# Gathering one chunk of every eleventh group with SyncE in two softmax passes of a graph network

## The chip, the cores and the metric

The kernel runs on one core of a Trainium2 chip as a single launch. The metric is the device time of one execution in microseconds, the median of several. PE is TensorE (PEld its weight loads), DVE VectorE, ACT ScalarE, POOL GpSimd and SP SyncE.

## The reference, cut to what matters

Four graph layers run over 6250 nodes with 128 features and 100,000 edges, each followed by a residual sum and a layer norm. The change touches layers 1 and 2. Both fetch one row per edge from a table that is indexed by the edge's source, take a softmax over the edges of each destination, and sum the weighted rows per destination:

```python
# layer 1 (eight heads; keys kt and values vt by edge type)
kt = jnp.einsum('nhi,thij->tnhj', k, relation_att)[edge_type, src]
e = (q[dst] * kt).sum(-1) * relation_pri[edge_type] * scale
m = jax.ops.segment_max(e, dst, num_segments=n)
ex = jnp.exp(e - m[dst])
a = ex / jax.ops.segment_sum(ex, dst, num_segments=n)[dst]
vt = jnp.einsum('nhi,thij->tnhj', v, relation_msg)[edge_type, src]
agg = jax.ops.segment_sum(a[..., None] * vt, dst, num_segments=n)
# layer 2 (four heads; one table x_l)
e = jax.nn.leaky_relu(x_l[src] + x_r[dst], NEG_SLOPE)
logits = jnp.einsum('ehc,hc->eh', e, att)
...
out = jax.ops.segment_sum(alpha[:, :, None] * x_l[src], dst, num_segments=n)
```

## The kernel before

The kernel sorts the edges by destination and pads them to 832 chunks (`CH`) of 128 edges. Four chunks (`G`) make a group, so a pass has 208 groups (`GROUPS`). `read_order` reads the sorted list back and makes, for each chunk, a column of row numbers: `by_dst.typed` (edge type times 6400 plus source, for layer 1) and `by_dst.other` (the source, for layer 2).

`softmax_pass` is one block of straight code per engine, unrolled over the groups. In layer 1 a fetched row has 256 floats (keys and values, from the table `related`), in layer 2 it has 132 (from `left_table`). The queues divide the work in this way:

- POOL issues one indirect DMA per chunk (L1505), four per group, into `rows`, a ring of 11 groups in layer 1 and 15 in layer 2. Before group n it waits until DVE has weighed group n - ring, which DVE does at the end of its step n - 1.
- DVE runs one step per group: it makes the one-hot matrix of group n (L140), multiplies group n - 2 with its spread queries (L1788 in layer 1, L1791 in layer 2), reduces to scores (L1814), weighs an older group (L1877) and adds older sums to `total` (L1694). Every `wg` groups (4 in layer 1, 8 in layer 2) a window's running maximum is formed by scans on DVE and small transposes on PE, and this work is spread over the steps of the following window.
- PE transposes the one-hots, spreads the queries (L1582; in layer 2 it also adds the fetched rows, L1585, and so waits for the gather itself) and sums the weighted rows (L1610). ACT casts between them.
- SP loads the break table in 32 DMAs (64 in layer 2) at the pass's start (L1479), and then, in layer 1, waits for the last score and reloads `k.x` (L1492). Nothing else stands on its queue.

A group's four gathers count on one semaphore, `got[slot]`, which the readers await at a fixed multiple. Each DMA adds 16 to its semaphore. All numbers of a wait are fixed when the program is built.

Of the kernel before, what the change touches and what calls it, by code (L numbers as in the profile page):

```python
# [5 lines left out]
ALU = mybir.AluOpType  # L6
# [4 lines left out]
I32 = mybir.dt.int32  # L11

P = 128
# [8 lines left out]
G = 4  # L22
# [14 lines left out]
GROUPS = CH // G  # L37
# [9 lines left out]
SPAN = TU + NBLK  # L47
assert PAD_STEP * (CH - 1) + PAD_SKIP * (P - 1) < N
AFTER = NSLOT - E
assert TU * QU == CU and RING * G == 64 and NBLK < (RING - 2) * G  # L50

NBD = NBLK + NBLK % 2
NPD = NBD * P
# [75 lines left out]
def load_blocks(nc, engine, chunk, count, most=NBLK - 1):  # L129

    _, regs = nc.values_load_multi_w_load_instructions(
        chunk, engines=[engine], min_val=0, max_val=most,
        skip_runtime_bounds_check_because="the table is clamped to the last block")
    return regs
# [596 lines left out]
                pool.wait_ge(sent[s], 64 * (groups // SLOTS))  # L731


def read_order(nc, k, table, o, breaks, fields, name, stack=None, shared=None):


    with ExitStack() as own:
# [5 lines left out]
        starts = sb("starts", [TQ, QT, P])  # L743
        breaks_sb = sb("breaks_sb", [TQ, QT, P], BF16)
        end = sb("end", [1, P], BF16)
        outs = [out for _, out in fields] + [o.begins]
        turned = ps("turned", [P, 4, 512])
        loaded = [sem(f"loaded{h}") for h in range(2)]
# [12 lines left out]
        @block.sync  # L761
        def _(sp):
            for h in range(2):
                here = slice(h * half, (h + 1) * half)
                sp.dma_start(lst[:, here, :], rows[:, here, :]).then_inc(loaded[h], 16)
            sp.dma_start(before[:], rows_before).then_inc(led, 16)
            sp.wait_ge(ended, 1)
            sp.dma_start(breaks[NSLOT:NSLOT + P].rearrange("(a b) -> a b", a=1), end[:]).then_inc(stored, 16)
            sp.wait_ge(flagged, 2)
            sp.dma_start(breaks[0:NSLOT].rearrange("(q p e) -> p q e", q=QT, e=P), breaks_sb[:]).then_inc(stored, 16)  # L770
            sp.wait_ge(stored, 32)

        @block.tensor
        def _(pe):
# [584 lines left out]


def softmax_pass(nc, k, o, index, table, row, head, values_at, spread, att, peaks, total, reload, loops, wg, name, beside=(),
                 ringed=False):

# [18 lines left out]
    with ExitStack() as ctx:  # L1384
# [71 lines left out]
        rescaled = sem("rescaled")  # L1456
        reloaded = sem("reloaded")
        kept = sem("kept")
        block = ctx.enter_context(nc.Block())
        slots = GROUPS + lag + 2  # L1460
        last_own = GROUPS + 1 - lag
# [12 lines left out]
        @block.sync  # L1474
        def _(sp):
            for n, here in enumerate((slice(0, batch), slice(batch, windows))):
                count = here.stop - here.start
                for s in range(strips):
                    sp.dma_start(brk[s * heads:(s + 1) * heads, here, :],  # L1479
                                 brk_h[s * length:s * length + NSLOT].rearrange("(a w l) -> a w l", a=1, l=wch * P)  # L1480
                                 [:, here, 0:length + 1].to_broadcast([heads, count, length + 1])).then_inc(loaded[n], 16)
            for tile, home, inward in beside:
                sp.dma_start(*((tile, home) if inward else (home, tile))).then_inc(kept, 16)
            for n in range(GU if ringed else 0):
                sp.wait_ge(got[n % RING], (n // RING + 1) * 16 * G)
                sp.sem_inc(landed, 1)
            if beside:
                sp.wait_ge(kept, 16 * len(beside))
            if reload is not None:
                tile, home = reload  # L1490
                sp.wait_ge(scored, GROUPS)
                sp.dma_start(tile, home).then_inc(reloaded, 16)  # L1492
                sp.wait_ge(reloaded, 16)

        @block.gpsimd
        def _(pool):
            for n in range(GU if ringed else GROUPS):
                s = n % ring
                if n >= ring:

                    pool.wait_ge(weighed if at else scored, n - ring + 1 + (NBLK // G if ringed else 0))
                    pool.sem_inc(running, 1)
                for g in range(G):
                    c = n * G + g
                    nc.gpsimd.indirect_dma_start(rows[:, s, g, :], None, table,  # L1505
                                                 bass.IndirectOffsetOnAxis(ap=index[:, c:c + 1], axis=0),
                                                 ).then_inc(got[s], 16)
# [48 lines left out]
        def _(pe):  # L1556
# [4 lines left out]
            for n in range(slots):  # L1561
# [10 lines left out]
                if 0 <= t < GROUPS:  # L1572
                    b = t % 2
                    blocks = load_blocks(nc, pe.engine, o.block[:, t * G:(t + 1) * G], G)

                    pe.wait_ge(copied, t + 1)
                    if t >= 2:
                        pe.wait_ge(paired, t - 1)
                    if att is not None:
                        pe.wait_ge(got[t % ring], (t // ring + 1) * 16 * G)  # L1580
                    for g in range(G):
                        last = nc.tensor.matmul(own[:, b, g, :], onehot_t[:, b, g, :], spread[:, bass.ds(blocks[g], 1), :],  # L1582
                                                start=True, stop=(att is None))
                        if att is not None:
                            last = nc.tensor.matmul(own[:, b, g, :], k.ident[:], rows[:, t % ring, g, 0:D],  # L1585
                                                    start=False, stop=True)
                    last.then_inc(spread_ok, 1)
# [74 lines left out]
        def _(dve):  # L1662
# [33 lines left out]
            for n in range(slots + 1):  # L1696
# [2 lines left out]
                m = n - lag  # L1699
                if n >= GROUPS + 2:  # L1700
                    add_sums(n - lag - 2)
                if n < GROUPS:
                    if n >= hots:

                        dve.wait_ge(widened, n - hots + 1)
                    mark(nc, onehot[:, n % hots, :, :], numbers, o.place[:, n * G:(n + 1) * G]).then_inc(hot, 1)
# [61 lines left out]
                if 0 <= t < GROUPS:  # L1768
                    b = t % 2

                    if ringed:
                        slots_of = load_blocks(nc, dve.engine, o.slot[:, t * G:(t + 1) * G], G, RING * G - 1)
                        need = dve.value_load(o.need[:, t:t + 1], min_val=1, max_val=GU)
                        dve.wait_ge(landed, need)
                    else:
                        dve.wait_ge(got[t % ring], (t // ring + 1) * 16 * G)
                    dve.wait_ge(spread_ok, t + 1)
                    if t >= 2:
                        dve.wait_ge(scored, t - 1)
# [1353 lines left out]
def graph_network(nc, a, out):  # L3133
    k = Shared()
    k.semaphores = []
    with ExitStack() as ctx:
        def sb(name, shape, dt=F32):
            return ctx.enter_context(nc.sbuf_tensor(f"k_{name}", shape, dt))
# [23 lines left out]
        by_src.gather = sb("src_gather", [P, CU], I32)  # L3162
        by_src.slot, by_src.need = sb("src_slot", [1, CH], I32), sb("src_need", [1, GROUPS], I32)
        by_src.free = sb("src_free", [1, 2 * P], I32)
        by_dst.typed = sb("dst_typed", [P, CH + SPARE], I32)
        by_dst.other = sb("dst_other", [P, CH + SPARE], I32)
        relational = ctx.enter_context(ExitStack())
# [9 lines left out]
        with ExitStack() as sort:  # L3177
# [51 lines left out]
            with unblocked as dense:  # L3229
                def tmp(name, shape, dt=F32):  # L3230
# [28 lines left out]
                swap_in(nc, k, queries, x_home, shared, "l1_swap")  # L3259
                read_breaks(nc, k, by_src.sorted, by_src, by_src.breaks, "src_breaks", dense, shared)  # L3260
            read_order(nc, k, by_dst.sorted, by_dst, by_dst.breaks,
                       [(1, by_dst.other), (2, by_dst.typed), (0, by_dst.place)], "dst_read")
            free_semaphores(nc, k)
        with ExitStack() as layer:
            total = layer.enter_context(nc.sbuf_tensor("l1_total", [P, NBLK - 1 + G, D + HEADS1], F32))
            softmax_pass(nc, k, by_dst, by_dst.typed, related.rearrange("t n f -> (t n) f"), 2 * D, D // HEADS1, D,
                         k.x, None, False, total, (k.x[:], x_home), None, 4, "l1_pass")
            relation_output(nc, k, total, a["L1_gnn_w_basis_a"], a["L1_gnn_loop_weight"], a["L1_gnn_bias"], mix,
                            "l1_out")
        relational.close()  # L3270
# [3 lines left out]
        with ExitStack() as layer:  # L3274
            def tmp(name, shape, dt=F32):
                return layer.enter_context(nc.sbuf_tensor(f"l2_{name}", shape, dt))

            right = tmp("right", [P, NBD, D])
            total = tmp("total", [P, NBLK - 1 + G, D + 2 * HEADS2])
            left = total[:, 0:NBD, 0:D + HEADS2]  # L3280
            loop_scores = tmp("loop_scores", [P, NBD, HEADS2])
            norm_project(nc, k, w2[:], None, [(0, D + HEADS2, left, 1.0), (D + HEADS2, 2 * D + HEADS2, right, 1.0)], [(left, left_table)], "l2_project")
            softmax_pass(nc, k, by_dst, by_dst.other, left_table, D + HEADS2, D // HEADS2, 0, right, att_row[:], True, total,
                         None, (left, loop_scores, k.x[:], bias2[:]), 8, "l2_pass")
            attention_output(nc, k, total, loop_scores, left_table, "l2_out")

        free_semaphores(nc, k)
# [44 lines left out]
```

## Time and profile before

| | |
|---|---|
| median of 3 runs | 9749.5 us (9728.2 to 9752.75) |
| profiled execution | 9737.26 us, span of its trace 9735.5 us |
| POOL busy | 6993.0 us (72%) |
| DVE busy | 6539.5 us (67%) |
| PE busy | 6374.2 us (65%) |
| ACT busy | 2118.1 us (22%) |

The span is cut into stretches by lines of the program: layer 1's pass runs from about 5188 to 6275 us and layer 2's from about 6429 to 7500 us. A line of a group gives the engine, the operation and its count, the duration of one in ns (least, median, most) and when the first and the last started. Lines indented under it say what ended the engine's idle time before it, or who waited for it, with the sum in us and the number of times. A name that ends in q (SPq, PEldq) is that engine's instruction queue: DMA issues and register instructions stand there and are not counted as busy.

### The profile page before, as it was taken

The numbers are of one execution on the slowest core, as the hardware profiler recorded it, in microseconds if no ns is written. First come the engines' busy times: TensorE is split into PE (matmuls) and PEld (weight loads), VectorE is DVE, ScalarE is ACT, GpSimd is POOL, SyncE is SP. The second block draws the span as 40 slices with busy tenths as digits, with TensorE's granted clock in tenths as the row PEclk, the third lists the DMA queues.
The fourth block names the chain that finished last, engine by engine and source line by source line (L and its number), as shares of the span: only waits on it lengthen the run. The fifth ranks groups of instructions, "written<-read, shape, count | busy, mean of one in ns | idle before, by whom it ended". The sixth has DMA issues, their size and how long they took to land. (4 is left out here: it accounts for less than half of the span.)

```text
span 9735.5 us, 171552 instructions
## 1 busy us (share of the span) xinstructions
PE 6374.2 (65%) x37681; PEld 5551.4 (57%) x37682; DVE 6539.5 (67%) x22695; ACT 2118.1 (22%) x6216; POOL 6993.0 (72%) x7418
## 2 busy tenths in 40 slices
PE   6777655547666577639404666767776688876666
PEld 5666544436655566634204666556675578766665
DVE  7555566668777777736305888877777666667777
ACT  5222100001111111112101222232222222223333
POOL 7777777767777777777776777547775577767775
PEclk7555555556666655569756888889999665667777
DMA  0000012122212212234303333222222322223333
GB/s 25 2 2 2 18 53 52 53 61 53 53 53 55 57 53 53 53 77 146 100 2 86 104 104 104 87 47 55 55 55 55 100 54 54 54 72 108 108 108 97
DMA packets 436037, 614.74 MB, mean 63 GB/s; under 512 B 176561, under 2 KB 312069, under 8 KB 435109
## 3 DMA queue, kind: packets, MB, share of 16 engines
q0 software_dynamic: 257024, 486.93, 19.6%
q1 hardware_dynamic: 178305, 119.49, 4.3%
q8 instruction: 183, 3.00, 0.1%
q10 hardware_dynamic: 292, 3.41, 0.1%
q14 instruction: 233, 1.91, 0.1%
HBM read 520.17 MB, written 89.19 MB: 63 GB/s over the span
## 5 line engine op out<-in xcount | busy, mean ns | idle before, releaser
L1179 PE MATMUL hop_sums<-hop_rows,hop_weighted 128*128 x4992 | 1152.1, 403 | 1053.2 <-SPq L1315 674.4
L1128 POOL DMA_INDIRECT hop_rows<-hops,k_src_gather x1568 | 1483.3, 946 | 486.8 <-issue 477.6
L1179 PEld LDWEIGHTS hop_sums<-hop_rows,hop_weighted 128*128 128x128 f32 x4992 | 989.6, 295 | 1158.8 <-issue 1158.7
L1505 POOL DMA_INDIRECT l_pass_rows<-left_table,k_dst_other x832 | 796.2, 957 | 433.2 <-issue 244.6
L1505 POOL DMA_INDIRECT l_pass_rows<-related,k_dst_typed x832 | 788.6, 948 | 308.6 <-issue 238.7
L1505 POOL DMA_INDIRECT l_pass_rows<-key_table,k_src_gather x784 | 744.3, 949 | 365.9 <-issue 234.8
L2000 POOL DMA_INDIRECT l_weigh_rows<-row_table,l_weigh_ring x832 | 790.0, 949 | 297.9 <-issue 213.1
L728 POOL DMA_INDIRECT src_sorted<-src_scatter_records,src_scatter_places x784 | 753.1, 961 | 260.4 <-issue 188.2
L1355 POOL DMA_INDIRECT dst_sorted<-rec,dst_places x768 | 752.8, 980 | 237.2 <-issue 237.2
L1128 POOL DMA_INDIRECT hop_rows<-in_x,k_src_gather x784 | 742.4, 947 | 249.0 <-issue 238.7
L1213 DVE TENSOR_SCALAR hop_weighted<-k_numbers,k_src_place,src_weight 128x128 f32<-128x128 f32 x2496 | 850.1, 403 | 15.7 <-issue 8.7
L1521 ACT CAST l_pass_onehot_t<-l_pass_turned 128x512 f32<-128x512 bf16 x624 | 365.7, 586 | 2158.6 <-PE l_pass_turned L1569 2110.8
L1600 PE MATMUL l_pass_sums<-l_pass_zero 128*128 128x272 bf16 (+1 forms) x1210 | 235.7, 279 | 465.2 <-DVE l_total L1694 322.0
L1582 PE MATMUL l_pass_own<-l_right,l_pass_onehot_t 128*128 x1664 | 359.0, 299 | 257.7 <-DMA l_pass_rows<-left_table,k_dst_other 243.8
L1610 PE MATMUL l_pass_sums<-l_pass_terms,l_pass_onehot_f 128*128 128x136 f32 x3232 | 513.1, 308 | 1.1 <-DVE l_pass_terms L1877 1.1
L664 PE MATMUL src_scatter_nexts<-src_scatter_next_sb,src_scatter_oh_lo_t 128*128 128x50 f32 x1568 | 494.2, 425 | 0.0
L1106 ACT COPY hop_next_sb<-hop_next_ps 128x50 f32<-128x50 f32 x784 | 158.1, 202 | 1522.6 <-PE hop_next_ps L1151 1516.5
L1610 PEld LDWEIGHTS l_pass_sums<-l_pass_terms,l_pass_onehot_f 128*128 128x128 f32 x3232 | 472.1, 217 | 26.3 <-issue 3.2
L2018 PE MATMUL l_weigh_own<-l_keys,l_weigh_onehot_t 128*128 x1672 | 321.5, 352 | 229.9 <-ACT l_weigh_onehot_t L1970 229.9
L1814 DVE TENSOR_REDUCE l_pass_scores<-l_pass_pair 128x32 f32<-128x512 f32 (+1 forms) x624 | 426.2, 683 | 14.5
L1582 PEld LDWEIGHTS l_pass_own<-l_right,l_pass_onehot_t 128*128 128x128 f32 x1664 | 267.1, 202 | 289.7 <-issue 289.7
L2018 PEld LDWEIGHTS l_weigh_own<-l_keys,l_weigh_onehot_t 128*128 128x128 f32 x1672 | 272.4, 247 | 274.6 <-issue 274.6
(477 smaller groups left out, 17048.9 us busy)
## 6 DMA issues: line engine op xcount, KB each, us to landing
related<-l_tables_rows SPq DMA_DIRECT2D x50, 1024.0 KB, 4.5
hop_rows<-hops,k_src_gather POOLq DMA_INDIRECT x1568
l_pass_rows<-related,k_dst_typed POOLq DMA_INDIRECT x832
l_pass_rows<-left_table,k_dst_other POOLq DMA_INDIRECT x832
l_weigh_rows<-row_table,l_weigh_ring POOLq DMA_INDIRECT x832
src_sorted<-src_scatter_records,src_scatter_places POOLq DMA_INDIRECT x784, 2.1
hop_rows<-in_x,k_src_gather POOLq DMA_INDIRECT x784, 2.5
dst_sorted<-rec,dst_places POOLq DMA_INDIRECT x784
```

The lines of the kernel that those rows point to most:

```text
L664: nc.tensor.matmul(nexts[:, b, g, 0:HIS], oh_lo_t[:, b, g, :], next_sb[:, g % 2, :], start=True, stop=True).then_inc(looked, 1)
L728: nc.gpsimd.indirect_dma_start(table, bass.IndirectOffsetOnAxis(ap=places[:, s, g:g + 1], axis=0), records[:, s, g, :], None).then_inc(sen ...
L1128: nc.gpsimd.indirect_dma_start(rows[:, s * G + g, :], None, table_in, bass.IndirectOffsetOnAxis(ap=o.gather[:, c:c + 1], axis=0),).then_in ...
L1179: last = nc.tensor.matmul(sums[:, b, g, :], weighted[:, s % SLOTS, g, :], rows[:, bass.ds(slots[g], 1), :], start=True, stop=True)
L1213: last = nc.vector.tensor_scalar(weighted[:, s, g, :], k.numbers, o.place[:, c], o.weight[:, c], ALU.is_equal, ALU.mult)
L1355: nc.gpsimd.indirect_dma_start(table, bass.IndirectOffsetOnAxis(ap=places[:, c:c + 1], axis=0), rec[:, c, :], None).then_inc(sent[c % SLOT ...
L1505: nc.gpsimd.indirect_dma_start(rows[:, s, g, :], None, table, bass.IndirectOffsetOnAxis(ap=index[:, c:c + 1], axis=0),).then_inc(got[s], 16)
L1582: last = nc.tensor.matmul(own[:, b, g, :], onehot_t[:, b, g, :], spread[:, bass.ds(blocks[g], 1), :], start=True, stop=(att is None))
L1610: last = nc.tensor.matmul(into[:, bass.ds(within[g], 1), 0:width], onehot_f[:, m % 2, g, :], term, start=False, stop=False, skip_group_che ...
L1814: nc.vector.tensor_reduce(mine, pair[:, b, :, :, :].rearrange("p (s t) h f -> p s t h f", t=per), AX.X, ALU.add).then_inc(scored, 1)
L2000: nc.gpsimd.indirect_dma_start(rows[:, s, g, :], None, table, bass.IndirectOffsetOnAxis(ap=ring[:, s, g:g + 1], axis=0),).then_inc(got[s], 16)
L2018: last = nc.tensor.matmul(own[:, b, g, :], onehot_t[:, b, g, :], spread[:, bass.ds(blocks[g], 1), :], start=True, stop=True)
```

## The change

Groups 16, 27, ... 203 of each pass (18 of 208) are side groups. POOL issues three gathers for them instead of four, 814 per pass in all. Their last chunk is fetched by SP: it loads the chunk's 128 row numbers from DRAM into `side_list`, takes eight at a time into registers, and issues 128 DMAs of one row each into `side`, a tile with two buffers. At step n of a side group DVE waits for the 128 rows and copies them to their place in `rows`; PE and DVE wait for this copy (`side_in`) before they use the group. SP may refill a buffer when DVE has copied the one before it. The row numbers by chunk come from `read_order`, where POOL computes them from the list and SP stores them in two DRAM tables.

```diff
+FIRST_SIDE, SIDE_STEP = 16, 11
+AT_ONCE = 8
...
# read_order, SP (after the breaks are stored) and POOL
-            sp.wait_ge(stored, 32)
+            sp.wait_ge(homed, 4)
+            for tile, home in ((other_i, other_home), (typed_i, typed_home)):
+                sp.dma_start(home.rearrange("(q p) e -> p q e", q=QT), tile[:]).then_inc(stored, 16)
+            sp.wait_ge(stored, 64)
+        @block.gpsimd
+        def _(pool):
+            for h in range(2):
+                pool.wait_ge(loaded[h], 16)
+                nc.gpsimd.tensor_copy(other_i[:, here, :], by_edge[:, here, :, 1]).then_inc(homed, 1)
+                nc.gpsimd.tensor_scalar(first_row[:, here, :], by_edge[:, here, :, 2], float(NPD), None, ALU.mult).then_inc(first_ok, 1)
...
+                nc.gpsimd.tensor_copy(typed_i[:, here, :], first_row[:, here, :]).then_inc(homed, 1)
# softmax_pass, SP
+            def list_side(j):
+                c = side_groups[j] * G + G - 1
+                sp.dma_start(side_list[:, j % 2, :], row_home[c:c + 1, :]).then_inc(side_listed[j % 2], 16)
+            for j in range(2 if side_groups else 0):
+                list_side(j)
+            for j, n in enumerate(side_groups):
+                b = j % 2
+                sp.wait_ge(side_listed[b], 16 * (j // 2 + 1))
+                if j >= 2:
+                    sp.wait_ge(side_in, j - 1)
+                for first in range(0, P, AT_ONCE):
+                    nodes = load_blocks(nc, sp.engine, side_list[:, b, first:first + AT_ONCE], AT_ONCE, table.shape[0] - 1)
+                    for e, node in enumerate(nodes):
+                        sp.dma_start(side[first + e:first + e + 1, b, :], table[bass.ds(node, 1), :]).then_inc(side_got[b], 16)
+                if j + 2 < len(side_groups):
+                    list_side(j + 2)
# softmax_pass, POOL
-                for g in range(G):
+                for g in range(G - 1 if n in side_groups else G):
# softmax_pass, PE before L1582 and DVE before L1788 and L1791
-                        pe.wait_ge(got[t % ring], (t // ring + 1) * 16 * G)
+                        pe.wait_ge(got[t % ring], gathered(t))
+                        if t in side_groups:
+                            pe.wait_ge(side_in, side_groups.index(t) + 1)
# softmax_pass, DVE at the start of step n
+                if n in side_groups:
+                    j = side_groups.index(n)
+                    dve.wait_ge(side_got[j % 2], (j // 2 + 1) * 16 * P)
+                    if n >= ring:
+                        dve.wait_ge(weighed, n - ring + 1)
+                    nc.vector.tensor_copy(rows[:, n % ring, G - 1, :], side[:, j % 2, :]).then_inc(side_in, 1)
```

On SP, from the end of `read_order` into layer 1's pass, these instructions stood in a row before (`x16` is a run of 16 alike; `dst_read_breaks_sb` are the breaks of the sorted list, `l_pass_brk` the pass's table of them):

```order
L770 DMA dst_breaks<-dst_read_breaks_sb 104x8x128
L737 UNCONDITIONAL_BRANCH
L1474 UNCONDITIONAL_BRANCH
L1479 DMA l_pass_brk<-dst_breaks 8x4x129 x16
L1479 DMA l_pass_brk<-dst_breaks 8x48x129 x16
L1492 DMA k_x<-x_home 128x6400
L1384 UNCONDITIONAL_BRANCH
```

Now the stores of the two tables and the row fetches stand between them; `ISA` is a register instruction that turns a row number into an address:

```order
L778 DMA dst_breaks<-dst_read_breaks_sb 104x8x128
L781 DMA dst_other_home<-dst_read_other_i 104x8x128
L781 DMA dst_typed_home<-dst_read_typed_i 104x8x128
L739 UNCONDITIONAL_BRANCH
L1510 UNCONDITIONAL_BRANCH
L1515 DMA l_pass_brk<-dst_breaks 8x4x129 x16
L1515 DMA l_pass_brk<-dst_breaks 8x48x129 x16
L1528 DMA l_pass_side_list<-dst_typed_home 1x128 x2
L133 TENSOR_LOAD l_pass_side_list
L1541 ISA
L1541 DMA l_pass_side<-related 1x256
L1541 ISA
```

The last two rows come 128 times per side group, with one load of eight numbers ahead of every eight, and 18 such blocks stand ahead of the reload of `k_x`.

On DVE, step 16 of layer 1's pass began in this way before:

```order
L1694 TENSOR_TENSOR l_total<-l_total,l_pass_sums 128x544
L131 TENSOR_LOAD k_dst_by_chunk
L1914 ISA
L1914 SCALAR_TENSOR_TENSOR l_total<-l_pass_small,l_total 128x128
L1917 ISA
L1917 SCALAR_TENSOR_TENSOR l_total<-l_pass_small,l_total 128x8
L140 TENSOR_TENSOR l_pass_onehot<-l_pass_numbers,k_dst_place 128x512
```

Now the copy out of the side tile stands ahead of the one-hot:

```order
L1751 TENSOR_TENSOR l_total<-l_total,l_pass_sums 128x544
L133 TENSOR_LOAD k_dst_by_chunk
L1980 ISA
L1980 SCALAR_TENSOR_TENSOR l_total<-l_pass_small,l_total 128x128
L1983 ISA
L1983 SCALAR_TENSOR_TENSOR l_total<-l_pass_small,l_total 128x8
L1765 COPY l_pass_rows<-l_pass_side 128x256
L142 TENSOR_TENSOR l_pass_onehot<-l_pass_numbers,k_dst_place 128x512
```

The one-hot, and all that DVE has queued behind it, moved behind the wait of this copy.

## Rows read from the trace of the kernel before

**Rows 1.** POOL's gathers, line L1505, in layer 1's pass, then layer 2's:

```profile
L1505 POOL DMA_INDIRECT l_pass_rows<-related,k_dst_typed x832: 941/949/985, 5188.4 to 6251.5; - x167
  issue: 238.7, 756
  DVE l_pass_terms L1877: 36.7, 75
...
  DVE l_pass_pair L1788: 20.2, 8
...
L1505 POOL DMA_INDIRECT l_pass_rows<-left_table,k_dst_other x832: 941/947/6695, 6429.9 to 7481.0; - x167
  DVE l_pass_terms L1877: 11.2, 31
...
  PE l_pass_own L1582: 243.8, 165
```

**Rows 2.** DVE's one-hots, line L140, steps 16 to 203, layer 1, layer 2:

```profile
L140 DVE TENSOR_TENSOR l_pass_onehot<-l_pass_numbers,k_dst_place x188: 672/680/684, 5268.9 to 6226.3; 128x512 bf16<-128x512 f32 x188
L140 DVE TENSOR_TENSOR l_pass_onehot<-l_pass_numbers,k_dst_place x188: 671/681/685, 6516.4 to 7455.1; 128x512 bf16<-128x512 f32 x188
```

**Rows 3.** Windows: busy us of PE, PEld, DVE, ACT, POOL; PEclk, DMA share, GB/s:

```profile
5269.00:6226.00 957.00, 668.91 (x4672) 601.55 (x4670) 773.31 (x1919) 247.71 (x655) 709.20 (x749) 0.84 0.36 104
6517.00:7455.00 938.00, 701.42 (x5886) 645.69 (x5886) 697.00 (x1493) 276.58 (x794) 707.87 (x749) 0.98 0.25 55
```

**Rows 4.** SP's waits: us in total, times, longest:

```profile
SPq L1492 <- DVE l_pass_scores L1814: 1019.8, 1, 1019.8
```

**Rows 5.** Lines of SP's, PE's and ACT's queues: DMA issues and register instructions:

```profile
L1479 SPq DMA_DIRECT2D l_pass_brk<-dst_breaks x32: 268/298/308, 6429.2 to 6439.8; - x32
L1479 SPq DMA_DIRECT2D l_pass_brk<-dst_breaks x16: 264/301/363, 5187.7 to 5193.0; - x16
L2436 SPq FUSED_REGOPS  x50: 46/46/51, 4422.6 to 4732.1; - x50
L2436 SPq DMA_DIRECT2D related<-l_tables_rows x50: 372/372/409, 4422.7 to 4732.3; - x50
L1318 SPq TENSOR_LOAD <-k_src_free x540: 262/267/465, 1217.1 to 4126.8; - x180
L131 PEldq TENSOR_LOAD <-k_dst_by_chunk x1041: 326/331/345, 5198.0 to 9680.2; - x174
L1173 PEldq TENSOR_LOAD <-k_src_need x624: 305/310/322, 1198.8 to 4163.2; - x156
L295 ACTq DMA_DIRECT2D dst_sorted<-dst_load_pad x1: 305/305/305, 138.4 to 138.4; - x1
```

**Rows 6.** DMA queues (packets, MB, share), 5248:5249, 5249:5260, 6461:6462, 6462:6475, 6428:6441:

```profile
q1 hardware_dynamic: 20, 0.00, 2.2%
...
q0 software_dynamic: 424, 1.15, 35.8%
...
q1 hardware_dynamic: 10, 0.00, 1.1%
...
q0 software_dynamic: 307, 0.63, 22.0%
...
q1 hardware_dynamic: 375, 0.07, 2.6%
```

**Rows 7.** DMA issues: KB each, median us from issue to landing:

```profile
weights_att_column<-in_L_gnn_att SPq DMA_DIRECT2D x1, 0.5 KB, 2.2
```

**Rows 8.** DVE's groups by form: busy us, mean ns of one, idle:

```profile
L2727 DVE COPY l_right<-l_project_product 128x256 f32<-128x256 f32 x25 | 10.4, 414 | 0.0
```

**Rows 9.** POOL's own arithmetic, two lines, and SP's store of the breaks:

```profile
L347 POOL TENSOR_SCALAR src_count_oh_lo<-k_count,src_keys x196: 597/612/694, 15.4 to 131.0; 128x128 bf16<-128x128 f32 x196
L220 POOL IOTA src_load_slot_no<- 128x832 int32 x1 | 0.8, 827 | 0.7 <-POOLq L156 0.7
...
5183.68 0.30 SPq L770 DMA_DIRECT2D dst_breaks<-dst_read_breaks_sb  x1
5187.74 51.95 SPq L1479 DMA_DIRECT2D l_pass_brk<-dst_breaks  x32
```

More of the change, by code:

```diff
@@ L731, in _, with read_order @@
                 pool.wait_ge(sent[s], 64 * (groups // SLOTS))
-def read_order(nc, k, table, o, breaks, fields, name, stack=None, shared=None):
+def read_order(nc, k, table, o, breaks, fields, other_home, typed_home, name, stack=None, shared=None):
     with ExitStack() as own:
@@ L745, in read_order @@
         end = sb("end", [1, P], BF16)
+        other_i = sb("other_i", [TQ, QT, P], I32)
+        typed_i = sb("typed_i", [TQ, QT, P], I32)
+        first_row = sb("first_row", [TQ, QT, P])
+        homed = sem("homed")
+        first_ok = sem("first_ok")
+        row_ok = sem("row_ok")
         outs = [out for _, out in fields] + [o.begins]
@@ L770, in _ @@
             sp.dma_start(breaks[0:NSLOT].rearrange("(q p e) -> p q e", q=QT, e=P), breaks_sb[:]).then_inc(stored, 16)
-            sp.wait_ge(stored, 32)
+            sp.wait_ge(homed, 4)
[5 more added lines that the diff above has]
+            for h in range(2):
+                here = slice(h * half, (h + 1) * half)
+                pool.wait_ge(loaded[h], 16)
+                nc.gpsimd.tensor_copy(other_i[:, here, :], by_edge[:, here, :, 1]).then_inc(homed, 1)
+                nc.gpsimd.tensor_scalar(first_row[:, here, :], by_edge[:, here, :, 2], float(NPD), None, ALU.mult).then_inc(first_ok, 1)
+                pool.wait_ge(first_ok, h + 1)
+                nc.gpsimd.tensor_tensor(first_row[:, here, :], first_row[:, here, :], by_edge[:, here, :, 1],
+                                        ALU.add).then_inc(row_ok, 1)
+                pool.wait_ge(row_ok, h + 1)
+                nc.gpsimd.tensor_copy(typed_i[:, here, :], first_row[:, here, :]).then_inc(homed, 1)
         @block.tensor
@@ L1361, in softmax_pass @@
 def softmax_pass(nc, k, o, index, table, row, head, values_at, spread, att, peaks, total, reload, loops, wg, name, beside=(),
-                 ringed=False):
+                 ringed=False, row_home=None):
     heads = D // head
@@ L1458, in softmax_pass, with gathered @@
         kept = sem("kept")
+        side_groups = range(FIRST_SIDE, GROUPS, SIDE_STEP) if row_home is not None else ()
+        if row_home is not None:
+            side = sb("side", [P, 2, row])
+            side_list = sb("side_list", [1, 2, P], I32)
+            side_listed = [sem(f"side_listed{b}") for b in range(2)]
+            side_got = [sem(f"side_got{b}") for b in range(2)]
+            side_in = sem("side_in")
+        def gathered(n):
+            return sum(16 * (G - 1 if before in side_groups else G) for before in range(n % ring, n + 1, ring))
         block = ctx.enter_context(nc.Block())
@@ L1775, in _ @@
                     else:
-                        dve.wait_ge(got[t % ring], (t // ring + 1) * 16 * G)
+                        dve.wait_ge(got[t % ring], gathered(t))
+                        if t in side_groups:
+                            dve.wait_ge(side_in, side_groups.index(t) + 1)
                     dve.wait_ge(spread_ok, t + 1)
@@ L3164, in graph_network @@
         by_src.free = sb("src_free", [1, 2 * P], I32)
+        by_dst.other_home, by_dst.typed_home = dram("dst_other_home", [CH, P], I32), dram("dst_typed_home", [CH, P], I32)
         by_dst.typed = sb("dst_typed", [P, CH + SPARE], I32)
@@ L3261, in graph_network @@
             read_order(nc, k, by_dst.sorted, by_dst, by_dst.breaks,
-                       [(1, by_dst.other), (2, by_dst.typed), (0, by_dst.place)], "dst_read")
+                       [(1, by_dst.other), (2, by_dst.typed), (0, by_dst.place)], by_dst.other_home, by_dst.typed_home, "dst_read")
             free_semaphores(nc, k)
@@ L3266, in graph_network @@
             softmax_pass(nc, k, by_dst, by_dst.typed, related.rearrange("t n f -> (t n) f"), 2 * D, D // HEADS1, D,
-                         k.x, None, False, total, (k.x[:], x_home), None, 4, "l1_pass")
+                         k.x, None, False, total, (k.x[:], x_home), None, 4, "l1_pass", row_home=by_dst.typed_home)
             relation_output(nc, k, total, a["L1_gnn_w_basis_a"], a["L1_gnn_loop_weight"], a["L1_gnn_bias"], mix,
@@ L3283, in graph_network @@
             softmax_pass(nc, k, by_dst, by_dst.other, left_table, D + HEADS2, D // HEADS2, 0, right, att_row[:], True, total,
-                         None, (left, loop_scores, k.x[:], bias2[:]), 8, "l2_pass")
+                         None, (left, loop_scores, k.x[:], bias2[:]), 8, "l2_pass", row_home=by_dst.other_home)
             attention_output(nc, k, total, loop_scores, left_table, "l2_out")
```

## The prediction

> **What bounds the kernel now.** I read the line of the gathers on POOL in each pass first, because that is the work the change takes away, and its waits before its busy time. In both passes POOL issues 832 gathers of about 0.948 us with some 0.306 us of issue between two (244.6 us over 800, or 238.7 over 756), 1.25 us apiece and 5.0 us a group [rows 1]. The reader is to see who ends whose wait. In layer 2 PE waits 243.8 us, 165 times, for a gather to land, while POOL waits for DVE only 11.2 us. POOL's issue sets that pass. In layer 1 it is the other way round: POOL waits 75 times for DVE's weighing, 36.7 us in all, while DVE waits for gathers 8 times, 20.2 us [rows 1]. There DVE's chain of steps sets the pace.
>
> The steps of DVE say the same. From step 16 to step 203, the first and last side group, layer 1 takes (6226.3 - 5268.9)/187 = 5.12 us a step, more than POOL's 5.0; layer 2 takes (7455.1 - 6516.4)/187 = 5.02, POOL's pace [rows 2]. DVE is busy 773 of 957 us in the one and 697 of 938 in the other [rows 3]; layer 2 has room on DVE, layer 1 little. SP is free: in layer 1's pass it stands in one wait of 1019.8 us [rows 4].
>
> **What POOL gives back.** 18 x 1.25 = 22.5 us per pass is the most. In layer 2 it is all worth having if nothing else becomes late; in layer 1 it is worth nothing, since POOL already waits for DVE there.
>
> **What a side chunk costs SP.** This is the term that decides. Per row SP runs one register instruction and one DMA issue. The register instruction with multiplications takes 46 ns at L2436 [rows 5]. A DMA issue that need not wait for its predecessor took 264 and 268 ns, the least of the two runs of small issues; in the run of 32 most took 298 at a pitch of (6439.8 - 6429.2)/31 = 342 ns, so 44 ns lie between two instructions [rows 5]. With a register instruction between, each issue starts some 400 ns after the last, later than that pitch, so I take 270 ns and not 298. A row is 270 + 44 + 46 + 44 = 404 ns, and 128 rows are 51.7 us. The load of one number takes SP 267 ns; on PE four numbers take 331 where one takes 310, so eight cost about 49 more than one, 267 + 49 + 44 = 360 ns, 16 times 5.8 us. The issue of the next list is 0.3. A chunk costs SP C = 57.8 us.
>
> DVE's own pace for 11 steps is 11 x 5.12 = 56.3 us in layer 1 and 11 x 5.02 = 55.2 in layer 2. SP is the slower of the two by a little, and then DVE waits for SP at every side group, and everything behind DVE's copy in its queue (one-hot, products, weighing) waits, so PE, ACT and POOL too.
>
> Bounds for C, from the rows on both sides: if the register instruction hides behind the pitch, a row is 342 ns and C = 49.9; if every issue takes the 301 of the run of 16 (nearly the 305 of the one-partition store on ACT), a row is 435 and C = 61.8. A 128-partition issue took 372, another kind of transfer; it would make C = 70.9 and is the far end.
>
> A page would make it dearer. The Trainium skill, DMA: Bandwidth & Descriptors, section Latency and other measured facts, puts a register load at 600 ns at least; that would add 16 x 0.33 = 5.3 us to C and 36 x 5.3 = 191 us to the time. Here 540 loads on SP took 262 ns and up [rows 5], so the trace disagrees and I leave it out.
>
> **When SP can begin.** The row lists stand behind the break table in SP's DMA queue. In layer 1 the last packets of that queue move in 5248 to 5249 and none after 5249; in layer 2 the last move in 6461 to 6462 [rows 6]; q1 is SP's queue and has no row in the later windows. I begin the rows at 5249.5 and 6462.5, and add 2.2 us for the last row to land, as for a load of 0.5 KB [rows 7].
>
> **The sum.** If SP sets the pace, the copy of the last side group can start at begin + 18 C + 2.2.
> - Layer 1: 5249.5 + 1040.4 + 2.2 = 6292.1, against step 203 at 6226.3: 65.8 us later. DVE's own pace would be less: first rows at 5309.5 (a stall of 40.6 at step 16), then 17 x 56.7 us, to 6273.4. So SP decides, and +66.
> - Layer 2: 6462.5 + 1040.4 + 2.2 = 7505.1 against 7455.1: +50. POOL's 22.5 us are lost in this wait.
> - The copies: 128x256 took DVE 0.41 us out of another memory [rows 8]; 36 of at most that are 15 us, but all but one per pass lie inside the waits for SP. +0.5 us.
> - `read_order`: POOL runs eight passes over 512 numbers. The near rows are 827 ns for 832 numbers and 612 for 128 [rows 9], so 0.5 to 2.4 us each, 4 to 20 in all, in the shadow of DVE's work up to the store at 5183.68 or past it. Then two stores of 425 KB follow the store of the breaks, half that size, for which the block had 4.06 us up to the pass's first issue at 5187.74 [rows 9]. +1 to +10; I take +4, near the first row, which is a plain stream.
> - PE's and DVE's new waits on `side_in` stand two steps behind the copy and cost nothing. DVE's wait on `weighed` is for its own last step. The bytes fetched stay the same.
>
> Together 66 + 50 + 0.5 + 4 = +120 us. On the profiled execution's 9737.3 us (9735.5 of span and 1.8 around it) that is 9857; it ran 12 us under the median of 9749.5, so I predict 9870.
>
> **Rivals.**
>
> (a) SP keeps up. At C = 49.9 the first rows land at 5301.6 in layer 1, and DVE then goes at its own 56.7: 5301.6 + 963.9 = 6265.5, +39. In layer 2 they land at 6514.6, ahead of step 16 at 6516.4; POOL sets the pace and the whole 22.5 us are gained. With `read_order` +39 + 1 - 22.5 + 4 = +21, that is 9770, not slower than a measurement can tell. If POOL's relief counted in layer 1 as well, it would be -1, 9748. The point from which this case decides is C = 54 or less, 373 ns a row; for it speaks that a single issue can be as cheap as 264, against it that something has to stand between two. C = 54.4 gives +43 - 11 + 4 = +36.
>
> (b) One DMA ring is the limit, not SP's issue. Each row is one descriptor with its own completion. If these finish one behind the other in more than 404 ns, C is 128 times that. At 800 ns a row C = 102.4, and both passes end 18 x 44.6 us later still: 9870 + 1606 = 11,476. Against it: of the 32 small transfers with 384 packets (eight pieces and four counts each) 375 moved, with other ones', in the 13 us around their issue [rows 6], so transfers at 342 ns do not pile up there. But they may lie on several rings, and the rows show no transfer of one descriptor in a row of many. [...]
>
> (c) The side path is ready early and both passes are freed: -22.5 in each and +4, 9708. It needs the stall at step 16 of layer 1 gone, that is the first 128 rows in 19 us, 150 ns a row, under every row seen, and POOL's relief to count in layer 1, where POOL waits. I give it almost nothing.
>
> **How the numbers follow.** A measurement of this kernel can tell 0.3%, 29 us, from no change. SP as the bound with C from 54.4 to 62 (9785 to 10,020): 0.66. Still dearer issue, up to the far end, by hiccups or by 372 ns an issue: C = 66 gives 18 x 8.2 x 2 = 295 us more than the forecast, 10,165: 0.10. Rival (b): 0.08. Rival (a): 0.13. Rival (c): 0.03. Each us on C moves the time 36 us, and this makes the range: from 9770 (rival a) to 10,060 (C = 63), leaving the upper cases out. Slower by over 0.3%: 0.66 + 0.10 + 0.08 = 0.84; within: 0.13; faster: 0.03.
>
> **What would show it.** In the profile after, a row fetch on SP at a pitch of 400 ns and 18 blocks of some 58 us back to back; DVE's copy waiting for SP's DMA about 40 us at step 16 of layer 1 and about 5 in layer 2, then 1 to 3 us at each side group; POOL's waits for DVE grown in both passes; steps 16 to 203 about 983 us long in layer 1. The forecast is wrong if SP stands in its wait for `side_in` (it keeps up), if SP's blocks are short but the rows land late (ring), or if TensorE's granted clock, 0.98 of full speed in layer 2 [rows 3], falls towards its lower level of 1.2 GHz when PE idles more, which I have not priced.

## The result, and the profile after

The changed kernel takes 10,197.0 us, the median of 5 runs (10,192.6 to 10,198.8). The kernel before took 9744.2 us beside it (5 runs, 9728.2 to 9752.75). The ratio is 1.0464, 95% interval 1.0452 to 1.0476: 453 us slower. The forecast of 9870 us had the sign and the mechanism, and fell short of the size by almost three quarters of the loss. The profiled execution of the changed kernel took 10,198.8 us (its trace spans 10,197.1), 2 above the median; that of the kernel before, 9737.3 (9735.5), lies 7 below its own.

The steps of DVE come first, as in [rows 2]: its one-hots, steps 16 to 203, layer 1 and layer 2 (count, least/median/most ns of one, first and last start in us).

```profile
L142 DVE TENSOR_TENSOR l_pass_onehot<-l_pass_numbers,k_dst_place x188: 672/680/685, 5319.9 to 6462.1; 128x512 bf16<-128x512 f32 x188
L142 DVE TENSOR_TENSOR l_pass_onehot<-l_pass_numbers,k_dst_place x188: 671/681/692, 6763.7 to 7905.7; 128x512 bf16<-128x512 f32 x188
```

One of them takes what it took, 0.68 us, but the 187 steps last 1142.2 and 1142.0 us, where they lasted 957.4 and 938.7. The two layers had a pace of their own before; now both have the same one, 6.11 us a step or 67.2 us for eleven. Something that does not know the layer sets it. What DVE waits for stands under the copy of the side rows, with the idle time ahead of it and its number of waits:

```profile
L1765 DVE COPY l_pass_rows<-l_pass_side x36: 229/262/294, 5319.7 to 7905.5; 128x256 f32<-128x256 f32 x18, 128x132 f32<-128x132 f32 x18
...
  DMA l_pass_side<-left_table: 264.3, 18
  DMA l_pass_side<-related: 236.7, 18
```

DVE waits for SP's rows at every one of the 36 side groups, 501.0 us in all. The longest wait is at step 16 of layer 1; the waits of DVE in that stretch give it (total, times, longest), and below it the one of layer 2:

```profile
DVE l_pass_rows L1765 <- DMA l_pass_side<-related: 59.1, 2, 46.8
...
DVE l_pass_rows L1765 <- DMA l_pass_side<-left_table: 13.4, 1, 13.4
```

Then SP itself, in one block of 128 rows of layer 1, 5319 to 5387 us: the load of eight row numbers (L133) and what it runs for each row (L1541).

```profile
L133 SPq TENSOR_LOAD <-l_pass_side_list x17: 715/780/926, 5319.0 to 5386.3; - x17
...
L1541 SPq FUSED_REGOPS  x128: 37/37/37, 5319.8 to 5385.5; - x128
L1541 SPq MOVE l_pass_side<-related x128: 29/29/29, 5319.9 to 5385.6; - x128
L1541 SPq DMA_DIRECT2D l_pass_side<-related x128: 224/225/260, 5319.9 to 5385.6; - x128
```

The 128 rows go out in 65.7 us, and the 17th load is already the next block's: the blocks stand back to back, 67.2 us apart. A row starts 0.408 us after the last (median; 0.42 in the mean, with a gap of some 0.3 us more here and there). A load of eight takes 780 ns, and the two rows around it start 1.21 us apart, so it adds 0.80 us to the row's 0.408. POOL, relieved of 18 gathers a pass, stands and waits (line as in [rows 1], with the idle time ahead of it):

```profile
L1560 POOL DMA_INDIRECT l_pass_rows<-related,k_dst_typed x814: 942/949/1048, 5192.3 to 6486.7; - x163
...
  DVE l_pass_terms L1943: 279.6, 84
...
L1560 POOL DMA_INDIRECT l_pass_rows<-left_table,k_dst_other x814: 939/947/6763, 6664.0 to 7930.9; - x163
...
  DVE l_pass_terms L1943: 240.2, 55
```

Its waits for DVE grew from 36.7 to 279.6 us and from 11.2 to 240.2. The stretches of steps 16 to 203 in both layers (busy us of PE, PEld, DVE, ACT and POOL, then PEclk, DMA share and GB/s, as in [rows 3]):

```profile
5320.00:6462.00 1142.00, 707.26 (x4674) 632.37 (x4674) 776.85 (x1935) 247.72 (x655) 692.95 (x731) 0.76 0.31 87
6764.00:7906.00 1142.00, 733.54 (x5891) 674.05 (x5891) 699.63 (x1511) 276.58 (x794) 691.39 (x731) 0.88 0.20 46
```

Beside SP, no engine has much more to do than before. DVE, which now makes the copies, is busy 3.5 and 2.6 us longer. PE does the same matmuls in 38 and 32 us more, at a lower granted clock (0.84 to 0.76, 0.98 to 0.88 of full speed).

The loss adds up. From the start of a pass to its last score, layer 1 went from 1071.8 to 1303.9 us (+232.1) and layer 2 from 1057.4 to 1273.3 (+215.9); from `read_order`'s first load to layer 1's first issue it went from 21.96 to 28.98 (+7.0). That is 455 of the 461.6 us between the two traces; the medians are 453 apart. The other 6.6 lie in stretches that the change does not touch: what follows layer 2's last score took 2248.9 us before and 2260.5 after, and between 2251.6 and 2270.7 in five kernels of the experiments.

### The profile page after: what moved, and what is told of

The parts are those of the page before. It is cut to its first block and busy times, and to the rows that moved or that the text cites. A ratio compares the mean times of both kernels' runs of the same rounds, so it can differ in the third digit from the quotient of the medians.

```text
span 10197.1 us, 186120 instructions
## 1 busy us (share of the span) xinstructions
PE 6487.5 (64%) x37681; PEld 5652.8 (55%) x37682; DVE 6548.0 (64%) x22731; ACT 2118.3 (21%) x6216; POOL 6973.3 (68%) x7390
## 5 line engine op out<-in xcount | busy, mean ns | idle before, releaser
L1560 POOL DMA_INDIRECT l_pass_rows<-related,k_dst_typed x814 | 771.7, 948 | 534.2 <-DVE l_pass_terms L1943 279.6
L1624 PE MATMUL l_pass_turned<-k_identb,l_pass_onehot 128*128 128x128 bf16 x2496 | 302.7, 258 | 512.5 <-DVE l_pass_onehot L142 511.6
L1624 PEld LDWEIGHTS l_pass_turned<-k_identb,l_pass_onehot 128*128 128x128 bf16 x2496 | 210.2, 118 | 538.5 <-DVE l_pass_onehot L142 524.0
L1177 PE MATMUL hop_nexts<-hop_next_sb,hop_oh_lo_t 128*128 128x50 f32 x1568 | 439.0, 379 | 0.0
```

What stands on the lines that cost most here:

```text
L1177: nc.tensor.matmul(nexts[:, b, g, 0:HIS], oh_lo_t[:, b, g, :], next_sb[:, g % 2, :], start=True, stop=True).then_inc(looked, 1)
L1624: last = nc.tensor.transpose(turned[:, g, :], onehot[:, n % hots, g, :], k.identb[:])
```

## The experiments

The question was why a block costs SP 67.2 us and not 57.8, whether it is SP alone that holds the passes up, and what is left of the gain when SP does not. The kernel before took 9745.6 us (median) beside the first four and 9749.1 beside the last three.

**`mixed`: what a load costs by its size.** The side chunks load 1, 2, 4, 8 and 16 numbers at a time, in turn.

```diff
-AT_ONCE = 8
+SIZES = (1, 2, 4, 8, 16)
+                at_once = SIZES[j % len(SIZES)]
-                for first in range(0, P, AT_ONCE):
+                for first in range(0, P, at_once):
```

> The side blocks load their row numbers 1, 2, 4, 8 and 16 at a time, in turn from block to block; nothing else differs from the changed kernel. What makes a load of eight take 0.78 us where a load of one took 0.267? Theory A, the number of values: about 73 ns for each further value, so loads of 1, 2, 4, 8 and 16 take 0.27, 0.34, 0.49, 0.78 and 1.37 us, and blocks of 128 rows last about 92, 74, 69, 67 and 65 us. Theory B, a fixed price of a load that stands behind a DMA issue: all sizes take 0.7 to 0.8 us, and the blocks last about 158, 105, 80, 67 and 60 us.

It took 10,962.5 us (one run). SP's loads in the first five blocks of layer 1, sizes 1, 2, 4, 8 and 16:

```profile
L133 SPq TENSOR_LOAD <-l_pass_side_list x128: 429/495/597, 5236.4 to 5359.4; - x128
...
L133 SPq TENSOR_LOAD <-l_pass_side_list x64: 710/723/782, 5360.7 to 5462.7; - x64
...
L133 SPq TENSOR_LOAD <-l_pass_side_list x32: 458/558/611, 5464.7 to 5535.4; - x32
...
L133 SPq TENSOR_LOAD <-l_pass_side_list x16: 721/784/825, 5538.0 to 5600.6; - x16
...
L133 SPq TENSOR_LOAD <-l_pass_side_list x8: 1166/1229/1267, 5605.1 to 5660.8; - x8
```

Neither theory fits. A load of one, here behind a DMA issue, takes 495 ns and not the 267 of [rows 5], so more than the count is missing; and from 4 to 8 to 16 numbers each further number takes 56 ns ((784 - 558)/4 and (1229 - 784)/8), so it is no fixed price either. Size 2, at 723, is on no line with the others; why was not found out. From first to last row a block takes 123, 102.5, 72, 65.6 and 62 us: larger loads are cheaper per row, slowly.

**`nolook`: the rows without the lookup.** The same 128 DMA issues per block, from addresses fixed when the program is built; no loads.

```diff
-                    nodes = load_blocks(nc, sp.engine, side_list[:, b, first:first + AT_ONCE], ...)
-                    for e, node in enumerate(nodes):
-                        sp.dma_start(side[...], table[bass.ds(node, 1), :])...
+                    for e in range(AT_ONCE):
+                        node = (j * P + first + e) * 37 % 6250
+                        sp.dma_start(side[first + e:first + e + 1, b, :], table[node:node + 1, :])...
```

> Left out: the lookup of row numbers. SP fetches 128 rows at addresses fixed when the program is built, so there are no register loads and no address instruction on SP; the rows fetched are not those of the edges. Theory (SP's issue sets the passes): a row takes 0.27 to 0.34 us, a block 35 to 44 us, DVE waits for SP only at step 16 of layer 1 (about 17 us), layer 2 gains POOL's 22.5 us; in all about 9750 us, within 0.3% of before. Rival (one DMA ring, or the landing of rows, sets the pace): a block's rows still take about 67 us to land, and the time stays near 10,190 us. Rival (the copy and its waits in DVE's queue cost by themselves): over 9900 us with a short block.

It took 9747.1 us, ratio 1.000 (0.999 to 1.0009). SP's issues in the first block, and DVE's copies in the whole kernel:

```profile
L1541 SPq DMA_DIRECT2D l_pass_side<-related x128: 227/248/333, 5248.1 to 5285.7; - x128
...
L1765 DVE COPY l_pass_rows<-l_pass_side x36: 210/277/456, 5287.1 to 7451.2; 128x256 f32<-128x256 f32 x18, 128x132 f32<-128x132 f32 x18
...
  DMA l_pass_side<-related: 15.9, 1
```

A block takes 37.6 us, 0.295 a row, and all waits of the copies but the first of layer 1 are gone. The whole 453 us hang on the lookup, that is on the loads and on the register instructions of each row: the issues alone fit between the side groups, and rows at 0.295 us land without falling behind (the first copy begins 1.4 us after the block's last issue begins). The first copy's wait took most of what layer 2 won: its steps 16 to 203 took 920.5 us, 18.2 less than before.

**`step14`: the same price, asked for less often.** Every fourteenth group from 30 on, 13 a pass.

```diff
-FIRST_SIDE, SIDE_STEP = 16, 11
+FIRST_SIDE, SIDE_STEP = 30, 14
```

> Side groups 30, 44, ... 198: 13 per pass, every fourteenth group, all else as in the changed kernel. 14 steps are 70 to 72 us, more than the 67 us of a block. Theory (SP's issue sets the passes): DVE waits nowhere for SP; read_order's 7 us and 13 copies of 0.3 us in layer 1 against 13 x 1.25 = 16 us in layer 2: about 9739 us, within 0.3% of before. Rival (each side group costs by itself, 452 us over 36 of them, 12.6 us apiece): 26 x 12.6 = 327 us, 10,070 us.

It took 9737.3 us, ratio 0.9991 (0.9982 to 1.0001). SP's blocks are as long as in the changed kernel, 65.7 us, but 14 steps of DVE last 69 to 72 us, and no wait stands under the copies' line:

```profile
L1765 DVE COPY l_pass_rows<-l_pass_side x26: 220/283/437, 5330.9 to 7411.3; 128x256 f32<-128x256 f32 x13, 128x132 f32<-128x132 f32 x13
```

One pair of numbers turns 453 us of loss into no difference. Both were changed in one run: the later first group answers for the two first waits, 46.8 and 13.4 of the 501 us, and the spacing for the rest. A side group that need not wait costs next to nothing by itself; it is the ratio of SP's period to DVE's that decides.

**`nobody`: POOL's relief by itself.** POOL issues 814, and the side chunks are fetched and copied by no one (the kernel leaves that fetch out and works on the rows that lie there).

```diff
-                for first in range(0, P, AT_ONCE): ...   # SP's lists and rows
...
-                    nc.vector.tensor_copy(rows[:, n % ring, G - 1, :], side[:, j % 2, :])...
...
-                                pe.wait_ge(side_in, side_groups.index(t) + 1)
...
-                            dve.wait_ge(side_in, side_groups.index(t) + 1)
```

> Left out: the fetch of the side chunks and their copy. POOL issues 814 gathers per pass, SP and DVE do nothing for the side groups, whose last chunk is computed from old rows; read_order's additions stay. It measures what POOL's relief is worth at most. Theory: 22.5 us in layer 2, none in layer 1, where DVE's chain sets the pace, and read_order's 7 us on the other side: about 9729 us. Rival (POOL sets layer 1 too): 45 us, about 9706 us.

It took 9735.9 us, ratio 0.9991 (0.9981 to 1.0). DVE's steps 16 to 203 in both layers, and POOL's gathers of layer 1:

```profile
L142 DVE TENSOR_TENSOR l_pass_onehot<-l_pass_numbers,k_dst_place x188: 672/681/685, 5270.4 to 6227.6; 128x512 bf16<-128x512 f32 x188
L142 DVE TENSOR_TENSOR l_pass_onehot<-l_pass_numbers,k_dst_place x188: 671/682/687, 6518.1 to 7439.5; 128x512 bf16<-128x512 f32 x188
...
L1546 POOL DMA_INDIRECT l_pass_rows<-related,k_dst_typed x814: 941/949/1048, 5191.1 to 6252.9; - x163
...
  DVE l_pass_terms L1918: 53.6, 73
```

Layer 1 takes 957.2 us, as before, and POOL turns 16.9 of its 22.5 us into longer waits for DVE (36.7 to 53.6). Layer 2 takes 921.4, 17.3 us less, 0.96 per chunk and not 1.25; why not more was not found out. So the most that this change could bring, with the side path free of charge, is 17 us less `read_order`'s 7, some 0.1%. The median fell by 9.8 us, and its interval reaches 1.

**`sixteen`: fewer, larger loads.** Sixteen numbers at a time, all else as changed.

```diff
-AT_ONCE = 8
+AT_ONCE = 16
```

> Row numbers loaded 16 at a time in every block, else the changed kernel. In the run of mixed sizes such a block lasted 62 us against 65.6 with eight, so its period should be 63.3 us against 67.2. Theory (SP's period times 18, twice, is the time): 36 x 3.9 = 140 us less than the changed kernel, about 10,057 us. Rival (each side group costs DVE and PE by itself): no change, 10,190 us.

It took 10,075.9 us (two runs), ratio 1.0335 (1.0316 to 1.0354). The period is 63.9 us, 3.3 less (3.9 less was expected, and 140 us); 36 x 3.3 = 119 us, and the time fell by 121. The rule that the prediction gave, 36 us for each us on C, holds.

**`pairs`: a load behind a load.** Two loads of eight in a row, then sixteen rows.

```diff
-                for first in range(0, P, AT_ONCE):
-                    nodes = load_blocks(nc, sp.engine, side_list[:, b, first:first + AT_ONCE], AT_ONCE, ...)
+                for first in range(0, P, 2 * AT_ONCE):
+                    nodes = [node for lo in (first, first + AT_ONCE)
+                             for node in load_blocks(nc, sp.engine, side_list[:, b, lo:lo + AT_ONCE], AT_ONCE, ...)]
```

> Two loads of eight directly one behind the other, then 16 row fetches. Tells why a load of one takes 0.50 us behind a row fetch and took 0.267 elsewhere. Theory (a load stands about 0.23 us until the DMA issue ahead of it is done with): the first load of a pair takes 0.78 us, the second 0.55, and a block lasts 63.8 us. Rival (the price is that of eight values or of this tile): both take 0.78 us, and a block lasts 65.6 us as in the changed kernel.

It took 10,099.6 us (one run). The loads of layer 1 from 5264 to 5274 us are two pairs, 8 us apart: the first load of the first pair, then each pair (least/median/most):

```profile
L133 SPq TENSOR_LOAD <-l_pass_side_list x1: 786/786/786, 5264.5 to 5264.5; - x1
...
L133 SPq TENSOR_LOAD <-l_pass_side_list x2: 528/657/786, 5264.5 to 5265.3; - x2
...
L133 SPq TENSOR_LOAD <-l_pass_side_list x2: 521/652/784, 5272.5 to 5273.3; - x2
```

The same load of eight takes 786 and 784 ns behind a DMA issue, and 528 and 521 behind another load, so the price is not that of eight numbers alone. That the DMA issue ahead is the cause of all 260 ns between them, as the theory had it, is not shown, and `step14` speaks against it. There SP waits for `side_in` before some blocks, so that its last DMA issue lies further back. Here it ended 3.2 us before the load (first two lines; the third has the other 15 loads of the block, each behind a row's issue):

```profile
6857.31 0.24 SPq L1528 DMA_DIRECT2D l_pass_side_list<-dst_other_home  x1
...
L133 SPq TENSOR_LOAD <-l_pass_side_list x1: 690/690/690, 6860.7 to 6860.7; - x1
...
L133 SPq TENSOR_LOAD <-l_pass_side_list x15: 768/780/933, 6865.1 to 6923.4; - x15
```

Nine such loads, 0.5 to 3.2 us behind the last issue, took 683 to 691 ns. So an issue directly ahead comes to some 90 ns, and the other 160 or so are what a load saves by standing directly behind another load. Taken from the 267 of [rows 5], which also stands behind no issue, the 690 are 60 ns for each number past the first, near the 56 of `mixed`. But then one number behind an issue should cost some 360 ns, and it took 495 in `mixed`: the whole price of a load stays open.

**`layer2`: the side path only where POOL is the bound.** Side groups in layer 2's pass alone, 15 of them, and one list in `read_order`.

```diff
-AT_ONCE = 8
-FIRST_SIDE, SIDE_STEP = 16, 11
+AT_ONCE = 16
+FIRST_SIDE, SIDE_STEP = 20, 13
...
-            for tile, home in ((other_i, other_home), (typed_i, typed_home)):
+            for tile, home in ((other_i, other_home),):
... (POOL's sums for the other list go, too)
-        "l1_pass", row_home=by_dst.typed_home)
+        "l1_pass")
```

> Side groups in layer 2's pass alone, 20, 33, ... 202 (15 of them), row numbers 16 at a time; read_order makes only the list that layer 2 needs. SP's period is 63.3 us, a little under 13 steps of 5.0 less the saved gather, 63.8. Theory: layer 2 gains 15 x 0.95 = 14 us, layer 1 is as before, read_order costs 2 to 4 us: about 11 us or 0.1% under the kernel before, 9733 us. Rival (SP still the bound, or the relief eaten by DVE's copies): 9745 us or more.

It took 9735.9 us (11 runs), ratio 0.9986 (0.9977 to 0.9995), the only kernel here whose interval lies below 1, by 0.14% in the median. DVE's steps 16 to 203, as above, and its copies, under which no wait stands:

```profile
L142 DVE TENSOR_TENSOR l_pass_onehot<-l_pass_numbers,k_dst_place x188: 672/681/685, 5271.7 to 6229.2; 128x512 bf16<-128x512 f32 x188
L142 DVE TENSOR_TENSOR l_pass_onehot<-l_pass_numbers,k_dst_place x188: 671/682/686, 6520.1 to 7447.8; 128x512 bf16<-128x512 f32 x188
...
L1759 DVE COPY l_pass_rows<-l_pass_side x15: 210/224/363, 6540.3 to 7440.8; 128x132 f32<-128x132 f32 x15
```

Layer 2 takes 927.7 us instead of 938.7, 11 less where 14 were expected, and `read_order` costs 2.7 instead of 7.0. (The trace is of one of the longer of the 11 executions, 9749.8 us; its surplus lies behind layer 2, in the stretch of 2270.7 us named above.) In the medians it lies beside `step14`; one interval touches 1 and the other does not, which is all that can be said between the two.

## Why the prediction was right in kind and short in size

**The bound** was read rightly: POOL in layer 2, DVE's chain in layer 1. `nobody` shows both, layer 1 unmoved and layer 2 shorter. The 22.5 us for layer 2 were an upper end and came out at 17.3.

**SP as the new bound** was right: every one of the 36 copies waits for its rows, and both layers go at SP's pace. That SP would stand 1 to 3 us beyond DVE at each group was the size that failed: after the first of each pass the waits are (236.7 - 46.8)/17 = 11.2 and (264.3 - 13.4)/17 = 14.8 us.

**The step that failed is the term "What a side chunk costs SP", and in it the load.** Sixteen loads at 360 ns were to cost 5.8 us; at 0.80 each they cost 12.8, which is 7.0 of the 9.4 us by which C was short (67.2 for 57.8). The working had two faults of like size, both from the choice of rows. It started from 267 ns, the price of a load on SP that [rows 5] shows at L1318, behind a semaphore instruction and out of another tile; in `mixed`, behind a row's issue, a load of one takes 495, so 228 ns were missing. And it took what a further number costs from PE, (331 - 310)/3 = 7 ns, 49 for seven; in `mixed` eight numbers take 289 more than one (784 - 495), so 240 were missing. Why a load costs this much is not settled (`pairs`); that it does, and that it sets C, is shown. The rest of the 9.4 is 2.1 us in the rows and 0.3 in the list.

**The row** came out at 408 ns for 404, by luck, through faults that cancel: an issue of one descriptor takes 225 ns, not 270, the register instruction 37, not 46, but there is a MOVE of 29 ns between them that the sum did not have, with a gap of its own. The mean of 0.42 lies 16 ns over the forecast.

**The sum** then works: 36 us for each us on C is 36 x 9.4 = 338 us, with the 120 forecast 458, and 453 were measured. The stalls at step 16 were 46.8 us for 40.6 and 13.4 for about 5. The far end of the bounds, C = 70.9, held the value, but from a wrong cause (dearer issues); the range stopped at 63, and there it was too narrow: the loads were a price without a row of their own kind in the trace of before, and they got no bound.

**The page that was set aside.** The Trainium skill, DMA: Bandwidth & Descriptors, section Latency and other measured facts, puts a register load at some 600 ns at least. By the estimate from it the forecast would have been 9870 + 191 = 10,061. The runs show that it is no floor: 267 ns for one number at L1318, and 495 for one behind a row's issue. The eight here took 780, so 600 was nearer than 360, and the measurement lies past both.

**Rivals.** (a), SP keeps up, did not happen here, and `step14` and `nolook` show it where the price or the demand is less. (b), the ring: in the changed kernel a copy begins 1.2 us after the block's last issue, so the rows land as they are issued, and `nolook` shows the same at 0.295 us a row. The ring is not what limits here. SP's queue in a block of the changed kernel, 5320 to 5386 us (packets, MB, share of the time of 16 engines), says how far it is from that:

```profile
q1 hardware_dynamic: 252, 0.13, 0.8%
```

A row is two packets, one of 1024 bytes and one of 4. Their 0.8% of 16 engines would be 13% of one, if all lay on one.

(c) happened in no run: `nolook`, the nearest, still waits 15.9 us for its first block, and layer 1's steps 16 to 203 take 955.1 us where they took 957.4.

**`read_order`** cost 7.0 us, for +4 taken and +1 to +10 given. The timeline of POOL's last arithmetic there and of SP's stores (start, us):

```profile
5179.36 1.67 POOL L792 TENSOR_TENSOR dst_read_first_row<-dst_read_first_row,dst_read_lst 104x512 f32<-104x512 f32 x1
5181.09 0.61 POOL L795 CAST dst_read_typed_i<-dst_read_first_row 104x512 int32<-104x512 f32 x1
...
5183.53 0.30 SPq L778 DMA_DIRECT2D dst_breaks<-dst_read_breaks_sb  x1
5183.87 0.53 SPq L781 DMA_DIRECT2D dst_other_home<-dst_read_other_i  x1
5184.44 1.13 SPq L781 DMA_DIRECT2D dst_typed_home<-dst_read_typed_i  x1
5191.64 8.40 SPq L1515 DMA_DIRECT2D l_pass_brk<-dst_breaks  x20
```

POOL's arithmetic is done before SP's first store, at 0.6 to 2.0 us a step as bounded. The two stores and their landing put off the pass's first issue, from 4.06 us behind the first store [rows 9] to 8.11, so they are 4.0 of the 7.0. The other 3.0 lie ahead of that store, which came 20.9 us after `read_order`'s first load and not 17.9. They are DVE's: beside POOL's arithmetic three of its instructions take longer. Two of them, before and after:

```profile
5179.73 0.42 DVE L818 TENSOR_SCALAR dst_read_breaks_sb<-dst_read_starts 104x512 bf16<-104x512 f32 x1
5181.04 0.16 DVE L800 TENSOR_TENSOR dst_read_starts<-dst_read_lst,dst_read_before 104x4 f32<-104x4 f32 x1
...
5177.49 1.18 DVE L842 TENSOR_SCALAR dst_read_breaks_sb<-dst_read_starts 104x512 bf16<-104x512 f32 x1
5179.56 1.49 DVE L824 TENSOR_TENSOR dst_read_starts<-dst_read_lst,dst_read_before 104x4 f32<-104x4 f32 x1
```

The last of these starts while POOL's L792 runs and ends 0.02 us after it; its first turn went from 0.17 to 1.38 us in the same way. In `layer2`, where POOL makes only two conversions, one instruction is longer (0.92 us) and the stretch costs 0.75. So POOL's arithmetic did not lie in the shadow of DVE's work, as the prediction put it: it held that work up.

**The copies** took 0.29 and 0.23 us, less than the 0.41 taken, and lie in or behind waits. **The granted clock** fell as feared, to 0.76 and 0.88 (in `nolook`, without the waits, it was 0.83 and 0.98). Its price was not measured by itself; PE's 38 and 32 us lie in stretches that SP's period of 67.2 us a side group already fills, so they set nothing here.

## What to carry to other kernels

Work that is moved to an idle engine costs that engine's instruction time, and that stands in no busy row: add the period of the new path and of the loop it feeds, and where the two lie within a fifth of each other, price every instruction of the period from a row with the same neighbour on the same engine, or give it a wide bound. A path that lags by a little on each turn loses the lag on every turn (here 9.4 us missed, 36 times); asking for it less often (14 steps for 11) removes the loss at once. Work put on an idle engine can also slow a busy one beside it, as POOL's arithmetic did to DVE in `read_order`. And find the ceiling first: with the side path free, 17 us of 9745 was all there was to win, in one layer of two.

## What the runs showed of the hardware that was not expected

- On SP a load of eight numbers into registers took 784 ns directly behind a DMA issue, 683 to 691 behind a semaphore wait with the last issue 0.5 to 3.2 us back (`step14`), and 521 directly behind another load (`pairs`). One number took 495 behind an issue and 267 at L1318.
- A load's price grows with its count, 558, 784 and 1229 ns for 4, 8 and 16 numbers behind an issue; two numbers took 723, which nothing here explains.
- A DMA issue of one row of 1 KB with an address out of a register takes 225 ns on SP, less than the 264 of any issue in [rows 5]; with a fixed address 248.
- Rows to one partition each were fetched at 0.295 us apiece, one behind the other, and the last was used 1.4 us after its issue began (`nolook`).
- A TENSOR_TENSOR of 104 x 4 numbers took DVE 1.49 us instead of 0.16 while POOL worked through one of 104 x 512, and ended with it.
